# Second attention of a two-layer kernel: queries stacked and numerators moved by on-chip copies, sums inverted compactly and then spread, combining and LN by pairs

## The reference, cut to what matters

```python
x = x + _L0_xattn_ref(_layernorm(x), mask, ctx_2048, ctx_2048, wq, wk, wv, wo)
x = x + _L0_ffn_ref(_layernorm(x), wa, rg, rgb, rw1, rb1, rw2, rb2, sg, ...)   # 16 routed experts, top 2, and 2 shared
x = x + _L1_xattn_ref(_layernorm(x), ctx_2048, Wq, bq, Wk, bk, Wv, bv, Wo, bo)
x = x + _L1_ffn_ref(_layernorm(x), W_up, W_gate, W_down)
```

```python
q = einsum('oc,bct->bot', Wq, query) + bq      # k, v likewise from ctx, 32 channels
q = q * cos + rotate_half(q) * sin             # heads of width 8
scores = einsum('bhqd,bhkd->bhqk', q, repeat(k, 4)) / sqrt(8)
attn = softmax(scores)                         # over 256 keys
out = einsum('bhqk,bhkd->bhqd', attn, repeat(v, 4))
out = einsum('oc,bct->bot', Wo, out) + bo
```

## Time and profile before

| | us |
|---|---|
| three runs | 850.47, 855.85, 858.68 |
| profiled execution | 855.41, its span 853.6 |
| PE busy | 561.3 |
| DVE busy | 494.2 |
| ACT busy | 330.1 |
| POOL busy | 226.8 |
| DVE reductions for the maxima (L1673) | 163.7, 256 of 683 ns |
| DVE reciprocals of the spread sums (L1692) | 28.0, 16 of 1747 ns |
| idle DVE just before them | 34.1, ended by the reads of `pv_scratch` |
| POOL's 32 gathers (L759) | 30.8, 963 ns each |

### The profile page before, as it was taken

One profiled execution on the slowest core, in us unless ns is written; L12 is line 12 of the kernel. 1 busy time (PEld: TensorE's weight loads), 2 busy tenths in 40 slices (PEclk: granted clock), 3 DMA queues, 4 the chain that ended last, 5 costly groups with the idle time before them and its releaser, 6 DMA issues.

```text
span 853.6 us, 11688 instructions
## 1 busy us (share of the span) xinstructions
PE 561.3 (66%) x4241; PEld 328.8 (39%) x4241; DVE 494.2 (58%) x1047; ACT 330.1 (39%) x490; POOL 226.8 (27%) x276
## 2 busy tenths in 40 slices
PE   3697809657846676703256686797669866797457
PEld 1475707556625555602032232252233422352124
DVE  2357752857613777422766967856888567751242
ACT  1112135654202555500024454446445474346323
POOL 2003133753670000245232044040222200040013
PEclk9898959888857998855558878797889998696659
DMA  8932090142225877322524034202240021002100
GB/s 248 293 102 84 31 304 21 35 103 74 87 104 113 186 195 156 106 68 52 109 49 82 8 97 111 47 2 65 53 112 7 25 41 40 1 2 65 33 6 25
DMA packets 95764, 71.34 MB, mean 84 GB/s; under 512 B 41738, under 2 KB 91036, under 8 KB 94556
## 3 DMA queue, kind: packets, MB, share of 16 engines
q1 hardware_dynamic: 90155, 58.80, 28.3%
q0 software_dynamic: 3504, 11.54, 4.2%
q10 hardware_dynamic: 2048, 0.27, 0.2%
HBM read 34.67 MB, written 27.26 MB: 73 GB/s over the span
## 4 chain that ended last, share of the span: by engine, by line
PE 36%; DVE 21%; issue 15%; POOL 11%; DMA 9%; ACT 5%; SPq 2%; ACTq 1%; DVEq 0%; POOLq 0%
PE ps L973 34%; DVE M L1673 4%; POOL sorted_scratch L741 4%; POOL RW L759 3%; DMA pv_scratch<-wqkvo 2%; DVE RS L1692 2%; DMA q_scratch<-RS 2%; DMA RS<-pv_scratch 2%; DVE acc L1647 1%; PE ps L985 1%; DVE stats L1301 1%; DVE mags L1387 1%; DVE RS L1314 1%; DVE RS L1566 1%; POOL RS L795 1%
## 5 line engine op out<-in xcount | busy, mean ns | idle before, releaser
L1673 DVE TENSOR_REDUCE M<-ps 128x2 f32<-128x512 f32 x256 | 163.7, 683 | 56.4 <-PE ps L973 55.9
L911 ACT ACTIVATE RW<-ps 128x1024 f32<-128x1024 f32 x128 | 128.2, 1025 | 148.2 <-PE ps L973 142.7
L973 PE MATMUL ps<-RS 128*128 128x128 f16 (+3 forms) x912 | 94.0, 266 | 45.5 <-DMA RS<-sorted_scratch 17.4
L973 PEld LDWEIGHTS ps<-RS 128*128 128x128 f16 (+1 forms) x912 | 81.6, 128 | 58.1 <-DVE RS L1571 18.5
L973 PE MATMUL ps<-RW,Vs 128*32 128x256 f32 x1024 | 89.3, 479 | 17.2 <-ACT wqkvo L922 9.0
L973 PE MATMUL ps<-RS,RW 48*128 48x256 bf16 (+1 forms) x448 | 57.2, 309 | 21.6 <-DVE M L1673 20.6
L664 POOL TENSOR_SCALAR var<-mv 128x4 f32<-128x4 f32 x16 | 4.0, 248 | 243.9 <-DVE mv L1306 236.6
L973 PE MATMUL ps<-tmp,xrow 48*128 48x256 bf16 x256 | 31.2, 327 | 53.8 <-DVE M L1673 40.3
L795 POOL TENSOR_TENSOR RS<-RS,RW 128x512 f16<-128x512 f32 x32 | 36.8, 1154 | 71.4 <-ACT RW L958 71.4
L759 POOL DMA_INDIRECT RW<-expert_scratch,pos x32 | 30.8, 963 | 91.5 <-DVE acc L1647 54.5
L973 PE MATMUL ps<-RW,RS 50*128 50x512 bf16 (+1 forms) x224 | 46.2, 424 | 11.0 <-DMA RW<-mlo 7.8
(11 more groups left out here) (215 smaller groups left out, 1009.8 us busy)
## 6 DMA issues: line engine op xcount, KB each, us to landing
sorted_scratch<-zero SPq DMA_DIRECT2D x1, 6144.0 KB, 19.9
expert_scratch<-RS SPq DMA_DIRECT2D x24, 256.0 KB, 2.8
RS<-pv_scratch SPq DMA_DIRECT2D x32, 128.0 KB
q_scratch<-RS SPq DMA_DIRECT2D x16, 192.0 KB, 4.5
RW<-in_wg SPq DMA_DIRECT2D x6, 384.0 KB, 6.1
RW<-in_wu SPq DMA_DIRECT2D x6, 384.0 KB, 6.4
RW<-in_w SPq DMA_DIRECT2D x3, 768.0 KB, 7.5
acc<-in_x SPq DMA_DIRECT2D x4, 512.0 KB, 8.1
```

The source lines that it names most:

```text
L911: act.activation(PT[:, k, :, :].rearrange("p i k -> p (i k)"), tile("st", n, 2), ACT.Exp, scale=float(HD) ** -0.5)\
L973: return pe.matmul(out, lhsT, rhs, start=first, stop=last)
L1673: dve.tensor_reduce(M[:, 2 * p + kv // 2, at:at + 2], tile("smax", 2 * n + i).rearrange("p (a b) -> p a b", a=2), AX.X, ALU.max).then_inc( ...
```

## The change

Five things are altered.

1. The split query terms go from `qsplit` straight to QS by six copies of 64 KB for each element (SBUF to SBUF), without `q_scratch`.
2. `take` on SP copies the four rows of sums to a compact tile `inv` (128 partitions x 64) and the numerators by eight copies straight to `num`, now with 32 partitions (d, key head) for each of the four heads of a key head; `wo1` is loaded in this order by four DMAs. A new piece `inv` has DVE invert the 128x64 tile, SP store it to `inv_scratch`, wait, and read it back spread over d by eight DMAs. The products of `nd` are POOL's.
3. `combine` and `rows2` go by pairs of elements; the wait for gathered rows is one for each pair. For groups 1 to 3 POOL normalises, for group 0 DVE.
4. `gather` is a piece of its own: that of group 0 one unit earlier in the list, that of group 1 behind `q1 3`, those of groups 2 and 3 in the sixth step of the group two before.
5. The combining of group 0 stands behind the last expert unit, and `rows2 1` between the second and third query.

```diff
@@ experts()
-    among[LAST_ROUTED + 2] = [("combine", 0)]
-    among[LAST_ROUTED + 3] = [("rows2", 0)]
+    among[LAST_ROUTED + 1] = [("gather", 0)]
...
-    return p + [("q1", j) for j in range(GB)]
+    return p + [("combine", 0), ("combine", 1), ("rows2", 0), ("q1", 0), ("q1", 1), ("rows2", 1), ("q1", 2), ("q1", 3), ("gather", 1)]
@@ attention()
+        if g and o == 3 and going:
+            p += [("inv", 2 * g - 1)]
         if going and g + 1 < NG:
             if o == 0:
-                p += [("combine", g + 1)]
+                p += [("combine", 2 * (g + 1) + k) for k in range(2)]
             if o == 1:
-                p += [("rows2", g + 1)]
+                p += [("rows2", 2 * (g + 1) + k) for k in range(2)]
...
+            if o == 5 and g + 2 < NG:
+                p += [("gather", g + 2)]
         if g:
+            if o == 1:
+                p += [("inv", 2 * g - 2)]
             if o == 2:
                 p += [("nd", 2 * g - 2)]
...
-    p += [("pv", 2 * STEPS - 2), ("pv", 2 * STEPS - 1), ("take", STEPS - 1), ("o1", 2 * g), ("nd", 2 * g + 1)]
+    p += [("pv", 2 * STEPS - 2), ("pv", 2 * STEPS - 1), ("take", STEPS - 1), ("o1", 2 * g), ("inv", 2 * g + 1), ("nd", 2 * g + 1)]
@@ build()
+        inv = sb("inv", [P, PAIRS_C, 64])
-        qd = nc.dram_tensor("q_scratch", [B, TERMS, P, T], BF16, kind="Internal").ap()
-        ud = nc.dram_tensor("pv_scratch", [B // 2, 2, HD + 1, KV, KV, T], F32, kind="Internal").ap()
+        ud = nc.dram_tensor("inv_scratch", [B // 2, KV, 2, KV, T], F32, kind="Internal").ap()
+        def normalise_pair(eng, n):
+            for t in (2 * n, 2 * n + 1):
+                eng.tensor_scalar(xn3[:, t % GB, :], acc[:, t, :], mv[0][:, t, 0:1], rstd[0][:, t:t + 1], ALU.subtract, ALU.mult)\
+                    .then_inc(ln_done[0], 1)
@@ SP
+                    for q in range(KV):
+                        sp.dma_start(wo1[32 * q:32 * q + 32, :], a["wo1"].rearrange("(r q h) e -> q r h e", r=HD, q=KV)[q])\
+                            .then_inc(w_queries, 16)
@@ SP q1
                 sp.wait_ge(q_split, n + 1)
-                sp.dma_start(qd[n].rearrange("t p k -> p t k"), qsplit[:, j, :, :]).then_inc(q_stored[j], 16)
-                sp.wait_ge(q_stored[j], 16 * (g + 1))
...
-                flat = qd[n].rearrange("t (d h) k -> (t d) (h k)", h=H)
-                for r0, count in ((0, 3), (3, 2), (5, 1)):
-                    at = 64 * i + 8 * r0
-                    sp.dma_start(QS[g % 2][at:at + 8 * count, p, :, :].rearrange("r h k -> r (h k)"), flat[0:8 * count])\
+                for r, term in enumerate((0, 1, 2, 0, 1, 0)):
+                    at = 64 * i + 8 * r
+                    sp.dma_start(QS[g % 2][at:at + 8, p, :, :].rearrange("r h k -> r (h k)"), qsplit[:, j, term, :])\
                         .then_inc(q_stacked[j], 16)
@@ SP take
                 for q in range(KV):
-                    sp.dma_start(ud[t // KV, :, :, q, :, :].rearrange("i r h k -> r i (h k)"),
-                                 U[p][32 * q:32 * q + HD + 1, :, :, :].rearrange("r i h k -> r i (h k)")).then_inc(u_stored[p], 16)
-                sp.wait_ge(u_stored[p], 16 * KV * (g + 1))
+                    sp.dma_start(inv[32 * q:32 * q + 32, p, :], U[p][32 * q + HD:32 * q + HD + 1, :, :, :].rearrange("r i h k -> r (i h k)"))\
+                        .then_inc(sums_in[p], 16)
                 if g:
                     sp.wait_ge(*full("o1", 2 * (g - 1) + p))
-                for i in range(2):
-                    sp.dma_start(num[:, 2 * p + i, :], ud[t // KV, i, 0:HD].rearrange("r q h k -> (r q h) k")).then_inc(nd_in[p], 16)
-                    sp.dma_start(den[:, 2 * p + i, :], ud[t // KV, i, HD].rearrange("(o q) h k -> o (q h) k", o=1)
-                                 .broadcast_to([HD, H, T])).then_inc(nd_in[p], 16)
+                for q in range(KV):
+                    for i in range(2):
+                        sp.dma_start(num[32 * q:32 * q + 32, 2 * p + i, :], U[p][32 * q:32 * q + HD, i, :, :].rearrange("r h k -> r (h k)"))\
+                            .then_inc(num_in[p], 16)
+            def inverses(n):
+                g, p = divmod(n, PAIRS_C)
+                sp.wait_ge(den_inv, n + 1)
+                sp.dma_start(ud[n].rearrange("q i h (c k) -> (q i h c) k", k=64), inv[:, p, :]).then_inc(inv_stored, 16)
+                sp.wait_ge(inv_stored, 16 * (n + 1))
+                if g:
+                    sp.wait_ge(normed, 2 * (n - 2) + 2)
+                for q in range(KV):
+                    for i in range(2):
+                        sp.dma_start(den[32 * q:32 * q + 32, 2 * p + i, :], ud[n, q, i].rearrange("(o h) k -> o h k", o=1)
+                                     .broadcast_to([HD, KV, T])).then_inc(den_in[p], 16)
@@ POOL
-                        .then_inc(y_back, 16)
-            def combine(g):
-                if g == 0:
-                    gather(0)
-                if g + 1 < NG:
-                    gather(g + 1)
-            def rows2(g):
-                normalise(2, g)
+                        .then_inc(y_back[n // GB], 16)
+            def rows2(n):
+                pair = slice(2 * n, 2 * n + 2)
+                pool.wait_ge(ln_mv[0], NG + n + 1)
+                pool.tensor_scalar(var[0][:, pair], mv[0][:, pair, 1], LN_EPS, None, ALU.add).then_inc(ln_var[0], 1)
+                pool.wait_ge(ln_var[0], NG + n + 1)
+                pool.tensor_tensor(rstd[0][:, pair], var[0][:, pair], minus_half[:, 0:2], ALU.pow).then_inc(ln_rstd[0], 1)
+                if n >= 2:
+                    pool.wait_ge(ln_rstd[0], NG + n + 1)
+                    normalise_pair(pool, n)
+            def nd(n):
+                g, p = divmod(n, 2)
+                pool.wait_ge(num_in[p], 16 * 8 * (g + 1))
+                pool.wait_ge(den_in[p], 16 * 8 * (g + 1))
+                for j in (2 * p, 2 * p + 1):
+                    pool.tensor_tensor(num[:, j, :], num[:, j, :], den[:, j, :], ALU.mult).then_inc(normed, 1)
@@ DVE
-            def combine(g):
-                dve.wait_ge(y_back, 16 * 2 * GB * (g + 1))
+            def combine(n):
+                summed(2 * n)
+                g, p = divmod(n, PAIRS_C)
+                dve.wait_ge(y_back[p], 16 * GB * (g + 1))
...
+            def rows2(n):
+                if n < 2:
+                    dve.wait_ge(ln_rstd[0], NG + n + 1)
+                    dve.wait_ge(ln_mv[0], NG + n + 1)
+                    normalise_pair(dve, n)
-            def nd(n):
-                g, p = divmod(n, 2)
-                dve.wait_ge(nd_in[p], 64 * (g + 1))
-                for i in range(2):
-                    j = 2 * p + i
-                    dve.reciprocal(den[:, j, :], den[:, j, :]).then_inc(den_inv, 1)
-                    dve.wait_ge(den_inv, 2 * n + i + 1)
-                    dve.tensor_tensor(num[:, j, :], num[:, j, :], den[:, j, :], ALU.mult).then_inc(normed, 1)
+            def inverses(n):
+                g, p = divmod(n, PAIRS_C)
+                dve.wait_ge(sums_in[p], 16 * KV * (g + 1))
+                dve.reciprocal(inv[:, p, :], inv[:, p, :]).then_inc(den_inv, 1)
```

More of the change, by code:

```diff
@@ L68, in load_of @@
     return LOADS.index((kind, n, 0))
+SHARED_UNIT = {(n, e): i for i, (kind, n, e) in enumerate(UNITS) if kind == "shared"}
 LAST_USER = {load_of(i): i for i in range(len(UNITS))}
@@ L635, in down4 @@
                 sp.dma_start(a["out"][GB * g:GB * g + GB].rearrange("b s d -> s b d"), acc[:, GB * g:GB * g + GB, :]).then_inc(stored, 16)
[L637 removed]
+            does = dict(at=at, kv1=kv1, down=down, evict=evict, keys=keys, q1=q1, take=take, inv=inverses, down4=down4)
             for what, *n in PIECES:
```

51 lines of the change are left out of this document (25 added, 26 removed).

## The result

The changed kernel took 870.23 us (median of four runs, 867.92 to 870.47) against 854.8 us for the kernel before in the same comparison. The ratio is 1.0204, 95% interval 1.0154 to 1.0253: **slower by about 2%**, where 824 us had been forecast, and outside the range of 811 to 844. The profiled execution spans 868.4 us at a mean granted clock of 0.79, against 853.6 at 0.80: 14.8 us more.

The account below looks back on a forecast made before the run. DVE was taken to lead in group attention with PE close behind, DVE and waits to count at the second attention's start. Terms -17.0 - 2.0 - 8.4 - 3.3 - 1.0 = -31.7 from 855.4 gave 824 us; range 811 to 844.

Parts of the forecast that it names:

- start, to the third quartet of maxima: Start of second attention: first maximum 19.5 us earlier at 390.0, third quartet at 414.3 instead of 431.3; gain 17.0 us.
- row copies of the maxima: PE's 4.07 us wait for the copy issued at 455.97 shrinks with less traffic; -2.0 us (0 to -3).
- group 1, group 2: Its attention: 6.3 us less on DVE, two thirds counting since PE is close; -4.2 us (0 to -6.3).
- group 3: Its attention, with no normalising to move: 4.9 us less on DVE; -3.3 us (0 to -4.9).
- tail: Last take to products: products at 814.6 to 816.6 instead of 816.8; -1.0 us (-2.8 to +1.1).
- The high end that I kept: Query stacking at second attention's start: 8.2 us per query instead of 4.1, second query ready at 396.5, 6.5 us later.
- the rule of the Trainium skill: Stack copies: engines limited to those dividing both sides' outer sizes; target has eight rows, moving the sum toward 8.2 us.
- the stall of POOL: Before POOL's first reciprocal deviations at second attention's start: 7.22 us of "issue" stays, now behind eight gathers.
- (c): Copies into eight partitions at 4 us per 64 KB delay the first maximum by 40 us: 864 us; chance 0.06.
- (a): Path from take to projection binds each group, so groups give 0 instead of 11.7: 836 or 842 us; chance 0.20.
- (d): No change: gains before 409 lost to gathers and stalls, needing 32 us of further waits; chance 0.04.

Follow-up runs that it names:

- sums_act: The changed kernel with the four copies of the sums issued by ACT's queue instead of SP's; 871.2 us, ratio 1.0227.
- qu_old: The changed kernel with query stacks and the numerator and sum path as before, only the pairwise order left; 842.86 us, ratio 0.989.
- q_old2: The changed kernel with the query stacks alone as before, through q_scratch with three reads per query; 855.84 us, ratio 1.0082.

## Why the prediction was wrong

Stage by stage, the terms of the sum against the same lines of the two traces (negative is a gain). The adding line after the last projection of a group stands in the changed kernel's timeline as

```profile
645.43 0.75 DVE L1736 SCALAR_TENSOR_TENSOR acc<-ps,bo,acc 128x512 f32<-128x512 f32 x1 [6.78 <-PE ps L1006]
...
739.05 0.75 DVE L1736 SCALAR_TENSOR_TENSOR acc<-ps,bo,acc 128x512 f32<-128x512 f32 x1 [4.96 <-PE ps L1006]
```

| term | forecast | measured | read at (before, after) |
|---|---|---|---|
| start, to the third quartet of maxima | -17.0 | -11.5 | 431.3, 419.8 |
| row copies of the maxima | -2.0 | +3.7 | 461.90, 454.15 |
| group 1 | -4.2 | +9.1 | 539.05, 540.35 |
| group 2 | -4.2 | +6.1 | 638.08, 645.43 |
| group 3 | -3.3 | +2.2 | 729.52, 739.05 |
| tail | -1.0 | +3.7 | 818.08, 831.33 |
| last feed-forward | 0 | +1.5 | 853.6, 868.4 |
| sum | -31.7 | +14.8 | |

The sum is missed by 46.5 us, and 23.6 of them are in groups 1 and 2. Of the -11.5 at the start 1.2 are no gain of the change: this run came to its first gather that much earlier. The last feed-forward is the same work; its first part ran at a granted clock of 0.53 (838.8 to 845.3) where before it had 0.75 (825.6 to 831.4), after PE had stood still for 17.9 us instead of 13.0 before the last pair's projection.

**The step that failed is in groups 1 and 2: "SP issues four copies of the sums (0.5 each, the old price: 524.0), landed 525.9; DVE, free at 522.2, waits 3.7 us".** It starts the sums at the end of the take, as if SP's queue were free then. In the order of the work the key reads and the next group's first two queries stand ahead of the take on SP. Each query's stack had just been repriced from four issues to six, and they were never set against the take that follows. The measured wait is 11.94 us, and with the queue freed 3.81. The working priced SP by issue and never added its issues up where it moved past other users; at a group's end they are 12 x 0.66 + 2.5 + 5.8 + 0.45 + 5.4 = 22.1 us of issues between 506.6 and 530.2. Two thirds of DVE's savings were to count; in group 1 DVE saved some 5 us of work and stood still for 19.2 us at the reciprocal and the addition (11.94 and 7.22), against 2.0 before (1.87 and 0.12). sums_act divides the excess at the reciprocal: about half is the order of the queue, the other half fits transfers already under way, and the prediction had neither.

**The price of a copy, 0.36 us for an issue**, came from reads of q_scratch. The kernel before had nearer rows: ACT's row copies between partitions at 0.60 us an issue stand in the earlier trace rows. Measured, from one issue to the next, were 0.65 for a stack copy, 0.62 for a copy of sums, 0.69 to 0.72 for spreads and numerators. The landing, 1.9 us after the last issue, was ample for the four small copies of sums in the tail (1.3) and failed for a row of stack copies (6.9): they leave at 1.0 us or more each. Two queries' copies from 379.26 (forecast 380.1) held the first maximum until 394.70, against 390.0. The high end that I kept, 8.2 us for each query, was the nearer value: measured are 7.4 (14.8 us for two, from 379.26 to the first scores at 394.09). The sentence on the rule of the Trainium skill spoke for it, and here the rule was the better guide.

**What the copies hold up** was not priced at all. The gathers of group 1 were given 2.83 us to land; the fourth took 10. DVE idled 7.37 and 1.11 us there, forecast 5.5 and 2.5: nearly the same sum, but by luck, since the maxima before it came 4.7 us later than forecast and hid that much of the lateness. The row copies of the maxima were to gain from less traffic. They met the stack copies instead: PE waited 7.45 us, from 4.07, and 4.69 us in group 1 just before the late projection (537.70).

**The tail.** The stages came in the forecast's order. The numerators' issues, 5.8 us instead of 2.9, delay the store of the inverse, and the spreads take 5.5 us. 18.9 us against 15.4, forecast 14.4. "The high end" of 0.6 was too low.

**POOL's normalising** was taken at 0.72 us at most for a tile and took 1.2 to 1.5 (2.43 and 2.93 for two). It is hidden behind maxima, as said; no time is lost there.

**Right** were the pairwise order (qu_old alone gains 13.5 us by the profiles), the stall of POOL, 7.54 us for 7.2, with DVE's first normalising at 372.49 for 373.4, and, by two errors that cancel, the size of the wait with a free queue.

**The rivals.** (c) had the sign and the eight rows, but its price, 4 us a copy from 3.3 on, and its place, the first maximum, were not what happened: copies at 1.0 to 1.65 us sufficed, because their queue is shared and because they come again in every group. Its "Against" had worked out the right pace, 1.0 us for 64 KB, and used it to put the rival aside, while the sum went by 0.36. (a) had the kind of place, waits between take and projection, but reckoned with a loss of DVE's gain at most: it kept the path at 13.2 to 16.4 us, where in group 1 it took 23.4 (509.8 to 533.2, the end of the products), and PE came to the projection only at 538.24. The range ended at 844 because no case let the issues of one stage stand ahead of another's. (d) had named 32 us of overlooked waits as what no change would need, and a loss needs more; the groups' ends and the start have them.

What stays open: how much of the 1.65 us per doubled copy is the gathers' share (their stretch is the slow one, but no run leaves them out), why a packet into eight rows takes so long, why sums_act lost its lead in group 3, and how much the new numerator path costs with a free queue (3.5 us by the profiles, 10 by the ratios).

## What to carry to other kernels

When a change adds DMAs to a queue, list everything that this queue issues in the stage, in its own order, with the measured price of an issue, and look up what now stands ahead of the first copy that an engine waits for; here the order alone was worth 17 us. Price a copy within the chip by the nearest row of the same kind, and a row of copies by their pace, not by one landing. Moving a small copy to another queue spares it the issues ahead of it, not the transfers: in sums_act that left half of the excess. Of a change with several parts, try each alone: the pairwise order was worth having, and was hidden under two parts that lost.

## What the runs showed that was not expected

- A copy of 64 KB from 128 rows of 512 bytes into eight rows takes 0.61 us to issue while the queue is free, and 1.05 us once about seventeen have been issued in a row; twelve more of them, partly beside gathers, cost 1.65 us each. Splitting the copies over two queues changed the time from first copy to first maximum from 15.41 to 15.37 us, nothing.
- Indirect gathers issued beside such copies are used 10 us after their issue; 6.2 without the stack copies in the same place (q_old2), under 3 before.
- The same copies delay others on other queues: 4 KB row copies on ACT's queue (7.0 to 10.3 us of PE's waiting instead of 3.5 to 5.0) and the four copies of the sums (5.3 us after the last issue instead of 1.3).
- From one issue to the next it is 0.72 us for numerator copies of one block and 0.83 for those of two at once, for spreads 0.69 and 0.68: it does not go with the bytes.
